# Local attention on one core: the closing feed-forward product moved to the next repeat, and the gates behind the third tile's scores

## The chip, the core and the metric

The kernel runs on one core of a Trainium2 chip. The metric is the device time of one execution in microseconds (us). Five engines work in parallel, each with its own instruction queue: PE (TensorE, matrix products and transposes into PSUM), DVE (VectorE), ACT (ScalarE), POOL (GpSimd) and SP (SyncE, which here issues all data transfers). They meet only at semaphores; within one engine everything runs in the order written.

## What is computed

The program has two parts. The first (up to about 1171 us of the span) is a mixture layer that the change does not touch. The second is a transformer of 6 layers over 8 sequences of 512 tokens, width 128, with 16 heads of 64 and local attention in windows of 32 keys, of which each query window sees its own and the one before:

```
def attn_layer(x, Wqkv, qs, ksc, Wo):
    q, k, v = split(x @ Wqkv)                       # 16 heads of 64
    q = l2norm(q) * qs;  k = l2norm(k) * ksc
    q = rotate(q, scale);  k = rotate(k, 1 / scale)
    return local_attention(q, k, v) @ Wo            # window 32

def ffn_layer(x, g, bln, W1, b1, W2, b2):
    xn = layernorm(x) * g + bln
    a, gate = split(xn @ W1 + b1)
    return a * gelu(gate) @ W2 + b2

for i in range(6):
    x = attn_layer(shift_tokens(x), ...) + x
    x = ffn_layer(shift_tokens(x), ...) + x
```

## The kernel before

`transformer` (line 1199) does the second part. One repeat (here: a trip) is one sequence in one layer, `it = l * 8 + s`; the program loops over the 6 layers and has the 8 sequences written out, so 48 trips run, of about 67 us each. The residual stream of all sequences lies in `state`, channels on partitions. A trip works on four tiles of 128 tokens, `t` = 0 to 3.

Nothing is scheduled by a planner. The list `BODY` (line 190) is the order, written by hand, and **every engine walks the same list**: at each name it does its own share of the step or passes on. The names are:

- `qk.t.j`: product of tile `t` with one of four column blocks of the query and key weights (PE, line 1535). DVE multiplies it with the rotary tables into `cs` (L1749), ACT squares it (L1629), DVE sums the squares per head (L1703), POOL adds the two halves of `cs` (L1409).
- `n.t`: the norms of tile `t`: DVE's last sum of squares and a clamp (L1731), ACT's logarithm and exponential (L1612, L1613), then POOL scales four blocks into `qk` (L1418).
- `t.t.j`: PE transposes those blocks (L1540), ACT copies them to `qTl` and `kTl` (L1640, L1642).
- `v.t.j`: value products (L1535), copied by ACT to `vl` (L1631); SP moves rows of `vl` into `vw` (lines 1328 to 1342). At `v.3.1` POOL copies the next sequence's stream to `xw` (L1427).
- `sa.t`, `s.t.p`: mask and scores of a tile in two halves (PE, L1498 and L1464); DVE takes the maximum and subtracts it (L1761, L1716), ACT exponentiates (L1619).
- `w.t`: DVE sums and inverts (L1723, L1736), POOL weighs (L1435). `pt.t.k`: PE transposes the probabilities (L1545), ACT copies (L1645). `oa.t`, `o.t.p`: output products (L1479), copied by ACT (L1647).
- `y`: output projection (L1552), added to `state` by DVE into `xm` (L1767). `xt`, `xn`: the layer norm's transposes (L1558, L1568).
- `gate.c`, `up.c`: three chunks of the hidden products (L1573). ACT applies gelu to the gate (L1659), DVE multiplies with `up` into `hf` (L1787). `y2`: closing product of `hf` with `w2l` (L1577), added by DVE to `xm` and stored in `state` (L1790).

A trip is skewed: it runs projections and early tiles of its own sequence, while the third and fourth tile's attention (`t.3`, `s.3`, `o.2`, `o.3`), `y` and the feed-forward layer belong to the sequence before (`rest_at` picks its slot).

Results leave PE through a `Ring` of the 8 PSUM banks: each product takes the next bank, and PE first waits for the reader of the product eight places earlier in the list (`readers`, `take`). Moving a name thus also moves who waits for whom.

ACT's gelu is in another function table than exponential and logarithm; where they alternate, an `ACT_TABLE_LOAD` stands between. After the loop a second block works through `OF_LAST` (line 206), the rest of the last sequence; the steps `f.s` there add and store the output. Before the loop DVE clears `kTl` and `oTl` (L1685) and then writes `tiled` (L1690), for which PE waits.

## Time and profile before

| | us |
|---|---|
| median of three runs | 4505.05 |
| the three runs | 4504.26 to 4511.89 |
| the profiled execution, its own time | 4507.19 |
| its span from first to last instruction | 4505.3 |
| PE busy | 4309.6 (96%) |
| DVE busy | 3286.9 (73%) |
| ACT busy | 2757.4 (61%) |
| POOL busy | 2181.4 (48%) |

A busy PE is not a PE at its peak, since an f32 matmul's end is modelled and overlaps the next one's start. What a step costs PE is the distance from its start to the start of the next step. The mean granted clock of TensorE is 0.994 of full.

### The profile page before, as it was taken

How to read it: one execution, taken by the hardware profiler on the slowest of the kernel's cores; microseconds unless marked ns; L12 is line 12 of the kernel's file. 1: busy time of each engine (PE TensorE's matmuls, PEld its weight loads, DVE VectorE, ACT ScalarE, POOL GpSimd, SP SyncE). 2: the span in 40 equal slices, each digit the busy share in tenths (PEclk: the TensorE clock that was granted, in tenths of full speed). 3: DMA queues.
4: the chain of work that ended last, by engine and by line, in shares of the span. 5: the costliest groups of instructions: out<-in, count | busy, mean ns of one | idle time of the engine just before them, and what ended most of it. 6: DMA issues, size and time to landing. Idle time of an engine off the chain costs nothing. (4 is left out here: it accounts for less than half of the span.)

```text
span 4505.3 us, 172609 instructions
## 1 busy us (share of the span) xinstructions
PE 4309.6 (96%) x68826; PEld 2563.6 (57%) x68826; DVE 3286.9 (73%) x5789; ACT 2757.4 (61%) x5467; POOL 2181.4 (48%) x1993
## 2 busy tenths in 40 slices
PE   8999999998799999999999999999999999999998
PEld 4555555555455655655555555555555555556554
DVE  5666666665687777777777777777777777777775
ACT  4544555544566666666666666666666666666664
POOL 0000000000366666666666766666766766666763
PEclk9999999999999999999999999999999999999998
DMA  1000000000111112111121112211122111221112
GB/s 44 4 8 6 8 8 4 8 6 4 55 53 51 46 46 71 46 49 50 43 74 48 45 49 61 56 48 47 48 58 59 49 45 48 64 53 49 50 44 80
DMA packets 145061, 189.72 MB, mean 42 GB/s; under 512 B 34151, under 2 KB 66298, under 8 KB 144250
## 3 DMA queue, kind: packets, MB, share of 16 engines
q1 hardware_dynamic: 144250, 178.39, 14.6%
q8 instruction: 572, 9.37, 0.9%
q14 instruction: 239, 1.96, 0.1%
HBM read 29.39 MB, written 4.19 MB: 7 GB/s over the span
## 5 line engine op out<-in xcount | busy, mean ns | idle before, releaser
L1409 POOL TENSOR_TENSOR cs<-cs 128x512 f32<-128x512 f32 x768 | 977.4, 1276 | 534.0 <-DVE cs L1749 531.3
L1535 PE MATMUL psum<-wqkv,xw 128*128 128x512 f32 x2304 | 1191.2, 609 | 24.1 <-DVE tiled L1690 15.6
L1749 DVE TENSOR_TENSOR cs<-psum,rots 128x1024 f32<-128x1024 f32 x768 | 933.8, 1221 | 236.6 <-PE psum L1535 225.5
L1418 POOL TENSOR_TENSOR qk<-cs,rn 128x512 f32<-128x512 f32 x768 | 776.6, 1042 | 330.3 <-ACT rn L1613 294.6
L1629 ACT ACTIVATE sq<-psum 128x512 f32<-128x512 f32 x768 | 459.0, 598 | 623.4 <-DVE cs L1749 591.8
L1442 POOL MEMSET tiled<- 128x128 bf16 x1 | 0.2, 204 | 1165.3 <-POOLq L524 1165.3
L1703 DVE TENSOR_REDUCE ss<-sq 128x8 f32<-128x512 f32 x768 | 520.0, 677 | 7.0
L1479 PEld LDWEIGHTS psum<-pT,vw 64*64 64x64 f32 x18624 | 400.4, 135 | 194.6 <-issue 194.2
L1540 PEld LDWEIGHTS psum<-ident,qk 128*128 128x128 f32 x3088 | 355.2, 141 | 230.6 <-issue 166.8
L1535 PEld LDWEIGHTS psum<-wqkv,xw 128*128 128x128 f32 x2304 | 368.6, 190 | 188.2 <-issue 164.4
L1540 PE MATMUL psum<-ident,qk 128*128 128x128 f32 x3088 | 444.9, 277 | 24.6 <-POOL qk L1418 17.8
L1479 PE MATMUL psum<-pT,vw 64*64 64x32 f32 x18624 | 445.4, 221 | 12.3 <-issue 11.0
L1435 POOL TENSOR_TENSOR probl<-probl,rs 128x512 f32<-128x512 f32 x386 | 394.4, 1043 | 52.3 <-DVE rs L1736 52.1
L1479 PE MATMUL psum<-pT,vl 64*64 64x32 f32 x6208 | 394.0, 219 | 0.0
L1464 PEld LDWEIGHTS psum<-kTl,qTl 64*32 64x32 f32 x24704 | 304.1, 105 | 147.8 <-issue 136.4
L1464 PE MATMUL psum<-kTl,qTl 64*32 64x64 f32 x24704 | 345.4, 223 | 12.6 <-issue 12.4
L1552 PE MATMUL psum<-oTl,wol 128*128 128x512 f32 x784 | 351.2, 601 | 0.6 <-DVE cs L1758 0.5
L1761 DVE TENSOR_REDUCE negmaxl<-psum 128x8 f32<-128x512 f32 x386 | 248.3, 685 | 128.1 <-PE psum L1464 127.8
L1619 ACT ACTIVATE probl<-probl 128x512 f32<-128x512 f32 x386 | 233.8, 629 | 161.4 <-DVE probl L1716 160.5
L1631 ACT COPY vl<-psum 128x512 f32<-128x512 f32 x384 | 223.0, 581 | 178.4 <-PE psum L1535 177.8
L1479 PEld LDWEIGHTS psum<-pT,vl 64*64 64x64 f32 x6208 | 326.3, 135 | 0.0
L1573 PE MATMUL psum<-x2T,w1l 128*114 128x512 f32 (+1 forms) x588 | 287.2, 612 | 0.4 <-ACT x2T L1635 0.4
(205 smaller groups left out, 6744.3 us busy)
## 6 DMA issues: line engine op xcount, KB each, us to landing
vw<-vl SPq DMA_DIRECT2D x768, 128.0 KB, 2.4
vw<-vl SPq DMA_DIRECT2D x672, 64.0 KB, 2.0
wqkv<-in_wqkv SPq DMA_DIRECT2D x42, 256.0 KB, 3.8
wol<-in_wol SPq DMA_DIRECT2D x7, 512.0 KB, 4.1
w1l<-in_w1l SPq DMA_DIRECT2D x7, 341.0 KB
xin<-in_x SPq DMA_DIRECT2D x9, 256.0 KB, 2.8
xr<-in_x SPq DMA_DIRECT2D x8, 256.0 KB, 2.8
sums<-sumout SPq DMA_DIRECT2D x8, 256.0 KB, 2.3
```

What stands on the lines that cost most here:

```text
L1409: summed_rot.done(nc.gpsimd.tensor_tensor(own, own, halves(cs[:, t % 2, j, 1, :])[:, :, ::-1, :], ALU.add), at)
L1418: rotated.done(nc.gpsimd.tensor_tensor(qk[:, j, :].rearrange("p (h c) -> p h c", c=EL), cs[:, t % 2, j, 0, :].rearrange("p (h c) -> p h c" ...
L1435: weighed.done(nc.gpsimd.tensor_tensor(p, p, r.unsqueeze(2).to_broadcast([P, 8, WK]), ALU.mult), (t, k))
L1464: last[p] = nc.tensor.matmul(banks[p][WIN * w:WIN * w + WIN, c * WK:(c + 1) * WK], qTl[rows, t % 2, c, WIN * w:WIN * w + WIN], kTl[rows, c ...
L1479: last[p] = nc.tensor.matmul(banks[p][64 * half:64 * half + 64, k * P + WIN * w:k * P + WIN * w + WIN], values(t, w, p)[:, c * EL:(c + 1) ...
L1535: last = nc.tensor.matmul(ps[:, :], xw[:, t * P:(t + 1) * P], wqkv[:, col:col + BANK], start=True, stop=True)
L1540: last = nc.tensor.transpose(ps[:, c * P:(c + 1) * P], qk[:, at[1], c * P:(c + 1) * P], ident[:, :])
L1552: last = nc.tensor.matmul(ps[:, :], wol[:, c, :], oTl[:, c, :], start=(c == 0), stop=(c == PAIRSL - 1))
L1573: last = nc.tensor.matmul(ps[0:CW[t], :], w1l[:, col:col + CW[t]], x2T[:, :], start=True, stop=True)
L1629: squared.done(nc.scalar.activation(sq[:, n % 2, :], ps[:, :], ACT.Square), at)
L1703: summed.done(V.tensor_reduce(ss[:, piece[0] % 2, 8 * j:8 * j + 8], sq[:, j % 2, :].rearrange("p (h c) -> p h c", c=EL), AX.X, ALU.add), p ...
L1749: parts.done(V.tensor_tensor(cs[:, t % 2, j, :, :].rearrange("p i (h c) -> p i h c", c=EL), twice, by_head, ALU.mult), at)
```

## The change

The closing product `y2` becomes `y2.0` and stands behind `qk.0.3 n.0` of the next trip; it closes the sequence before the one it closed until now, so it writes another slot (`closed_at`) and its weights `w2l`, `b2l` are loaded apart from the others, after it has read the old ones. At the top of the trip `t.3.3` and `qk.0.2` change places. At the end `v.3.1` goes ahead of the third tile's scores `s.2`, `n.3` directly behind them, and all three gates behind that. The last part gets one `y2` more, since two sequences are still open there. A third memset on DVE clears `hf`.

```diff
-MADE = 21
+MADE = 22
 BODY = [step(name) for name in """
-    qk.0.0 t.3.0 qk.0.1 t.3.1 t.3.2 qk.0.2 t.3.3 qk.0.3 n.0 pt.2.0 qk.1.0 sa.3
+    qk.0.0 t.3.0 qk.0.1 t.3.1 t.3.2 t.3.3 qk.0.2 qk.0.3 n.0 y2.0 pt.2.0 qk.1.0 sa.3
...
-    qk.3.3 sa.2 v.3.0 gate.0 s.2.0 s.2.1 gate.1 up.0 gate.2 v.3.1 w.2 oa.1
-    up.1 up.2 n.3 o.1.0 o.1.1 y2
+    qk.3.3 sa.2 v.3.0 v.3.1 s.2.0 s.2.1 n.3 gate.0 gate.1 w.2 up.0 gate.2 oa.1
+    up.1 up.2 o.1.0 o.1.1
...
-OF_LAST = (turn(3) + turn_probs(2) + score(3) + final(0) + [("w", 3)] + ...
-           + ... + hidden_chunks() + final(6) + [("y2",)] + final(7))
+OF_LAST = (turn(3) + [("y2", 0)] + turn_probs(2) + score(3) + final(0) + [("w", 3)] + ...
+           + ... + hidden_chunks() + final(6) + [("y2", 1)] + final(7))
...
+    def closed_at(l, s, which):
+        if which or s > 1:
+            return bass.ds(B - 1 if which else s - 2, 1)
+        past = (l * B + TRIPS - 1) // TRIPS
+        return bass.ds(B - past if s else B - past - past, 1)
+
+    closing_loads = lambda l, s: (l * B + s + B - 2) // B + 1
...
-            for j in range(1, 6):
+            for j in range(1, 4):
+                load_qkv(slice(0, 1), j)
+            load_closing(slice(0, 1))
+            for j in range(4, 6):
                 load_qkv(slice(0, 1), j)
...
-                left.wait(sp, it, "state")
+                hidden.wait(sp, it, 2)
                 settle(sp, passed)
                 load_ffn(one)
-                with sp.Fori(1, B - 1) as s:
+                move_values(it + 1, 0)
+                left.wait(sp, it + 1, (0,))
+                settle(sp, passed)
+                load_closing(one)
+                for t in range(1, T):
+                    move_values(it + 1, t)
+                with sp.Fori(2, B - 1) as s:
...
-                    left.wait_before(pool, it, "state")
+                    left.wait_before(pool, it, (0,))
...
-                if key == ("f", B - 1, 0):
-                    left.wait(pe, it, "state")
+                if key in (("f", B - 2, 0), ("f", B - 1, 0)):
+                    left.wait(pe, it, (at[0] - (B - 2),))
...
-                    hidden.wait(pe, it, 2)
+                    pe.wait_ge(w2_loaded, closing_loads(l, s) * (16 * W2_LOADS))
+                    wait_made(hidden, pe, it, 2, t == 0)
...
-                for dst in (kTl[:, :, :], oTl[:, :, :]):
+                for dst in (kTl[:, :, :], oTl[:, :, :], hf[:, :, :]):
                     V.memset(dst, 0.0).then_inc(made, 1)
-                dve.wait_ge(made, 11)
+                dve.wait_ge(made, 12)
```

How this moves instructions shows in the programs' own rows (source line, instruction, output and inputs, shape). Rows of line 77, 82, 134 and 151 are waits.

PE around the top of a trip, before; the first row is `y2`, the last ones stand ahead of `sa.3`:

```order
L1577 MATMUL psum<-hf,w2l 128x512 x3
L1535 MATMUL psum<-wqkv,xw 128x512
L1540 MATMUL psum<-ident,qk 128x128 x4
L1535 MATMUL psum<-wqkv,xw 128x512
L1540 MATMUL psum<-ident,qk 128x128 x8
L1535 MATMUL psum<-wqkv,xw 128x512
L1540 MATMUL psum<-ident,qk 128x128 x4
L1535 MATMUL psum<-wqkv,xw 128x512
L77 ISA
L1545 MATMUL psum<-ident,probl 128x128 x4
L1535 MATMUL psum<-wqkv,xw 128x512
L134 REGISTER_ALU x2
```

The same place after the change, from `qk.0.1` to the mask of `sa.3`:

```order
L1560 MATMUL psum<-wqkv,xw 128x512
L82 REGISTER_ALU
L1565 MATMUL psum<-ident,qk 128x128 x12
L1560 MATMUL psum<-wqkv,xw 128x512 x2
L77 ISA
L1600 REGISTER_ALU
L1603 MATMUL psum<-hf,w2l 128x512 x3
L1570 MATMUL psum<-ident,probl 128x128 x4
L77 REGISTER_ALU
L1560 MATMUL psum<-wqkv,xw 128x512
L134 REGISTER_ALU x2
L1523 MATMUL psum<-maskw,tiled 32x512 x8
```

The closing product moved from ahead of the trip's first product to between the four blocks of tile 0 and `pt.2.0`; the last transpose `t.3.3` moved one product up.

ACT near the end of a trip, before, from the copy of `v.3.0` to the second gelu:

```order
L1631 COPY vl<-psum 128x512
L77 REGISTER_ALU
L1659 ACT_TABLE_LOAD
L1659 ACTIVATE gel<-psum,b1l 114x512
L77 REGISTER_ALU
L1619 ACT_TABLE_LOAD
L1619 ACTIVATE probl<-probl 128x8x64
L77 REGISTER_ALU
L1619 ACTIVATE probl<-probl 128x8x64
L77 REGISTER_ALU
L1659 ACT_TABLE_LOAD
L1659 ACTIVATE gel<-psum,b1l 114x512
```

The same place after, from the copy of `v.3.1` to the first gelu:

```order
L1657 COPY vl<-psum 128x512
L77 REGISTER_ALU
L1645 ACTIVATE probl<-probl 128x8x64
L77 REGISTER_ALU
L1645 ACTIVATE probl<-probl 128x8x64
L77 REGISTER_ALU
L1638 ACTIVATE lns<-ssc 128x32
L151 REGISTER_ALU
L1639 ACTIVATE rn<-lns,lnt 128x32
L77 REGISTER_ALU
L1685 ACT_TABLE_LOAD
L1685 ACTIVATE gel<-psum,b1l 114x512
```

The exponentials and the norms of tile 3 now come first and the three gelus last, and two of four table loads are gone.

POOL in the same stretch, before, from the copy to `xw`:

```order
L1427 COPY xw<-state 128x513
L77 REGISTER_ALU
L1435 TENSOR_TENSOR probl<-probl,rs 128x512 x2
L77 REGISTER_ALU x2
L1418 TENSOR_TENSOR qk<-cs,rn 128x512
```

After:

```order
L1452 COPY xw<-state 128x513
L77 REGISTER_ALU x2
L1443 TENSOR_TENSOR qk<-cs,rn 128x512
L77 REGISTER_ALU
L1443 TENSOR_TENSOR qk<-cs,rn 128x512
L77 REGISTER_ALU
L1443 TENSOR_TENSOR qk<-cs,rn 128x512
L77 REGISTER_ALU
L1443 TENSOR_TENSOR qk<-cs,rn 128x512
L77 REGISTER_ALU
L1460 TENSOR_TENSOR probl<-probl,rs 128x512 x2
```

The scaling of tile 3 now stands ahead of the weighing of tile 2.

## Rows read from the trace of the kernel before

**Rows 1.** Stretch of 47 trips: length, busy time of each engine, clock, transfers.
```profile
1254.24:4441.16 3186.92, 3110.44 (x58369) 1879.88 (x58367) 2493.41 (x3924) 2083.99 (x3849) 2117.50 (x1926) 1.00 0.20 52
```
**Rows 2.** PE's waits in those trips: waiting line, releaser, total, times, longest.
```profile
PE psum L1498 <- ACT kTl L1642: 26.5, 46, 1.8
PE psum L1540 <- POOL qk L1418: 17.3, 70, 0.4
PE psum L1464 <- issue: 12.4, 27, 1.1
PE psum L1479 <- issue: 8.4, 20, 0.9
```
**Rows 3.** PE's timeline over one trip's turn: start, length, line, [idle before, releaser].
```profile
2391.13 1.88 PE L1535 MATMUL psum<-wqkv,xw 128*128 128x512 f32 x4
2392.94 0.41 PE L1498 MATMUL psum<-maskw,tiled 64*32 64x512 bf16 x8
...
2404.43 2.85 PE L1577 MATMUL psum<-hf,w2l 114*128 114x512 f32 x6
2407.11 1.02 PE L1535 MATMUL psum<-wqkv,xw 128*128 128x512 f32 x2
2407.97 0.60 PE L1540 MATMUL psum<-ident,qk 128*128 128x128 f32 x4
2408.40 1.02 PE L1535 MATMUL psum<-wqkv,xw 128*128 128x512 f32 x2
...
2412.73 1.02 PE L1535 MATMUL psum<-wqkv,xw 128*128 128x512 f32 x2
2414.28 0.41 PE L1498 MATMUL psum<-maskw,tiled 64*32 64x512 bf16 x8 [0.52 <-ACT kTl L1642]
...
2418.52 1.38 PE L1540 MATMUL psum<-ident,qk 128*128 128x128 f32 x8
...
2420.67 1.02 PE L1535 MATMUL psum<-wqkv,xw 128*128 128x512 f32 x2
```
**Rows 4.** DVE's timeline in the same stretch.
```profile
2398.07 1.28 DVE L1716 TENSOR_TENSOR probl<-psum,negmaxl 128x512 f32<-128x512 f32 x2
...
2407.31 1.51 DVE L1790 SCALAR_TENSOR_TENSOR state<-psum,b2l,xm 64x512 f32<-64x512 f32 x2 [2.18 <-PE psum L1577]
2408.86 2.36 DVE L1749 TENSOR_TENSOR cs<-psum,rots 128x1024 f32<-128x1024 f32 x2
...
2416.04 0.19 DVE L1731 TENSOR_TENSOR ssc<-ss,least 128x32 f32<-128x32 f32 x1
```
**Rows 5.** ACT's timeline in the same stretch.
```profile
2399.56 1.15 ACT L1619 ACTIVATE probl<-probl 128x512 f32<-128x512 f32 x2
2400.72 1.28 ACT L1659 ACT_TABLE_LOAD   x1
2402.02 1.27 ACT L1659 ACTIVATE gel<-psum,b1l 114x512 f32<-114x512 f32 x2
...
2405.42 0.32 ACT L1613 ACTIVATE rn<-lns,lnt 128x32 f32<-128x32 f32 x1
...
2413.46 0.58 ACT L1642 COPY kTl<-psum 128x512 f32<-128x512 f32 x1
```
**Rows 6.** POOL's timeline in the same stretch.
```profile
2405.96 4.05 POOL L1418 TENSOR_TENSOR qk<-cs,rn 128x512 f32<-128x512 f32 x4 [2.05 <-ACT rn L1613]
...
2417.08 4.05 POOL L1418 TENSOR_TENSOR qk<-cs,rn 128x512 f32<-128x512 f32 x4 [1.06 <-ACT rn L1613]
```
**Rows 7.** Timelines of DVE and PE ahead of the first trip.
```profile
1180.35 3.47 DVE L1685 MEMSET oTl<- 128x4096 f32 x1 [0.80 <-issue]
...
1185.74 2.07 PE L1535 MATMUL psum<-wqkv,xw 128*128 128x512 f32 x2 [15.62 <-DVE tiled L1690]
```
**Rows 8.** Timelines of SP and PE between the last trip and the closing part.
```profile
4442.32 0.54 SPq L1338 DMA_DIRECT2D vw<-vl  x1
...
4449.18 3.65 PE L1540 MATMUL psum<-ident,qk 128*128 128x128 f32 x16 [5.17 <-DVEq L66]
```

More of the change, by code:

```diff
@@ L203, in final @@
     return [("f", s, half) for half in range(2)]
-OF_LAST = (turn(3) + turn_probs(2) + score(3) + final(0) + [("w", 3)] + output(2) + final(1) + final(2) + turn_probs(3) + output(3)
-           + final(3) + [("y",), ("xt",)] + final(4) + [("xn",)] + final(5) + hidden_chunks() + final(6) + [("y2",)] + final(7))
+OF_LAST = (turn(3) + [("y2", 0)] + turn_probs(2) + score(3) + final(0) + [("w", 3)] + output(2) + final(1) + final(2) + turn_probs(3) + output(3)
+           + final(3) + [("y",), ("xt",)] + final(4) + [("xn",)] + final(5) + hidden_chunks() + final(6) + [("y2", 1)] + final(7))
 TRIPS = DEPTH * B
@@ L1187, in __init__ @@
         self.qkv_loaded = [ctx.enter_context(nc.semaphore(f"qkv_loaded{j}")) for j in range(6)]
-        self.o_loaded, self.ffn_loaded, self.rot_loaded, self.made = (
-            ctx.enter_context(nc.semaphore(n)) for n in ("o_loaded", "ffn_loaded", "rot_loaded", "made"))
+        self.o_loaded, self.ffn_loaded, self.w2_loaded, self.rot_loaded, self.made = (
+            ctx.enter_context(nc.semaphore(n)) for n in ("o_loaded", "ffn_loaded", "w2_loaded", "rot_loaded", "made"))
         self.vmoved = [ctx.enter_context(nc.semaphore(f"vmoved{t}")) for t in range(T)]
@@ L1203, in transformer @@
     mv, lnv, rstd, x2, x2T, gel, hf, qkv_loaded = buf.mv, buf.lnv, buf.rstd, buf.x2, buf.x2T, buf.gel, buf.hf, buf.qkv_loaded
-    o_loaded, ffn_loaded, rot_loaded, made, vmoved = buf.o_loaded, buf.ffn_loaded, buf.rot_loaded, buf.made, buf.vmoved
+    o_loaded, ffn_loaded, w2_loaded, vmoved = buf.o_loaded, buf.ffn_loaded, buf.w2_loaded, buf.vmoved
+    rot_loaded, made = buf.rot_loaded, buf.made
     def sem(name):
@@ L1240, in transformer @@
     hidden = steps("hidden", lambda key: key[1] if key[0] == "up" else None)
-    left = steps("left", last_of("y2", "state"))
+    left = steps("left", place("y2"))
     squared = steps("squared", place("qk"))
@@ L1285, in readers @@
             return [(hidden, at[0])]
-        return [(left, "state")]
+        return [(left, at)]
     ring = Ring(sem("filledl"), [(key, readers(key)) for key in order if key[0] not in ("n", "w", "sa", "oa")])
@@ L1312, in load_ffn @@
                 sp.dma_start(w1l[:, :], io["w1l"][layer].rearrange("l p n -> p (l n)")).then_inc(ffn_loaded, 16)
-                for dst, name in ((lng, "lng"), (lnb, "lnb"), (b2l, "b2l")):
+                for dst, name in ((lng, "lng"), (lnb, "lnb")):
                     sp.dma_start(dst[:, :], io[name][layer].rearrange("l p -> p l")).then_inc(ffn_loaded, 16)
@@ L1316, in load_ffn @@
                 for c, m in enumerate(CW):
-                    sp.dma_start(w2l[0:m, c, :], io["w2l"][layer][:, at:at + m, :].rearrange("l p d -> p (l d)")
-                                 ).then_inc(ffn_loaded, 16)
                     for a in range(2):
@@ L1321, in load_ffn, with load_closing @@
                                      .rearrange("l p -> p l")).then_inc(ffn_loaded, 16)
+                    at += m
+            def load_closing(layer):
+                sp.dma_start(b2l[:, :], io["b2l"][layer].rearrange("l p -> p l")).then_inc(w2_loaded, 16)
+                at = 0
+                for c, m in enumerate(CW):
+                    sp.dma_start(w2l[0:m, c, :], io["w2l"][layer][:, at:at + m, :].rearrange("l p d -> p (l d)")
+                                 ).then_inc(w2_loaded, 16)
                     at += m
@@ L1394, in _ @@
                 sp.wait_ge(qkv_loaded[j], DEPTH * 16 + 16)
-        FFN_LOADS = 4 + 3 * 3
+        FFN_LOADS, W2_LOADS = 3 + 2 * 3, 4
         @block.gpsimd
@@ L1790, in read @@
                     last = unshift(lambda a, b, d: V.scalar_tensor_tensor(
-                        out=state[a:b, rest_at(l, s), d:N + d].rearrange("p s n -> p (s n)"), in0=ps[a:b, :],
+                        out=state[a:b, closed_at(l, s, t), d:N + d].rearrange("p s n -> p (s n)"), in0=ps[a:b, :],
                         scalar=b2l[a:b, 0:1], in1=xm[a:b, d:N + d], op0=ALU.add, op1=ALU.add))
-                    left.done(last, "state")
+                    left.done(last, at)
             if last_part:
```

## The prediction

> **What bounds the kernel now.** I read three views in this order. First the table by stretches: over 47 trips, from the first product of the second trip to the start of the last closing product, PE is busy 3110.4 of 3186.9 us and DVE, the next, 2493.4, all at the full granted clock [rows 1]. So a trip takes 67.8 us, and only what PE executes and what it waits for count; an edit on another engine is worth nothing unless PE waits for it. Second PE's waits: two have an engine as releaser, the mask of `sa.3` for ACT's copy into `kTl` and the transposes `t.0.j` for POOL's scaled blocks; the others are "issue", PE waiting for nothing that the profile names, inside the long runs of small score and output matmuls [rows 2]. Third the timeline, to size the two. A pair of products with a mask behind takes 2392.94 - 2391.13 = 1.81, so one product with a mask behind takes 1.81 - 0.86 = 0.95, where 0.86 is a plain product (2407.97 - 2407.11). Ahead of `sa.3` it takes 2414.28 - 2412.73 = 1.55: **wait A is 0.60 us**. The three transposes `t.0.0` to `t.0.2` should take 3 x 0.435 = 1.31 (one is 2408.40 - 2407.97) and take 2420.67 - 2418.52 = 2.15: **wait B is 0.84 us** [rows 3]. The waits view counts less because it starts where a matmul's modelled end lies.
>
> **Why they are there.** DVE stands idle 2.18 us for the closing product, moves it out in 1.51 until 2408.8, and only then takes the first products of the trip, which PE had finished at 2407.97 and 2409.26 [rows 3, 4]. Everything behind is late by that: `cs`, ACT's squares, ACT's copy of `t.3.3`, which stands in ACT's queue behind the square of `qk.0.2` and ends at 2414.04 [rows 5], which is wait A, and the clamp of tile 0 at 2416.04 [rows 4], ACT's norm and POOL's four blocks from 2417.08 on, 1.01 us each [rows 6], which is wait B.
>
> **The change, top of the trip.** PE's work is the same 2.68 us (2407.11 - 2404.43 [rows 3]), in another place. I walk the new order in the trace's times. PE ends `o.1.1` at 2404.4 as before and starts `qk.0.0` at once. DVE, by then done with `hf`, takes the four products as they come: 2405.5, 2406.7, 2408.9, 2410.1 or soon after, with sums between, and has the clamp of tile 0 ready near 2413.4 instead of 2416.2. `t.3.3` leaves PE at 2407.9 and is no longer queued behind a square that is late; ACT has copied it by about 2410. `sa.3` comes at 2404.4 + four products, four transposes, 2.68, one transpose group and one product = 2413.6, over 3 us later: wait A is gone. DVE moves `y2.0` out from 2413.4 to 2414.9 and takes `qk.1.0` at 2414.9, 1.3 earlier than now. ACT's norm is out at 14.0, POOL's blocks end at 2415.1, 16.1, 17.1 and 18.1; PE wants the third at 2418.8: wait B is gone, with 1.7 in hand. `y2.0` itself waits for nothing: `hf` is complete at 2405.1, its weights were loaded a layer or a trip ago, its bank was freed by the square of `qk.0.0`, at 2407.3 against 2409.6. From there on every engine repeats the old schedule 1.44 earlier, since DVE is back to waiting for PE from `qk.1.2` on.
>
> **The change, end of the trip.** The new queue on ACT is exponentials, norm of tile 3, table load, three gelus, table load, two copies. The scores are centred at 2399.3 as now [rows 4]; the exponentials no longer wait for a table and end at 2399.9, the norm at 2400.9 (now 2405.7), the load at 2402.2, the gelus, 0.64 to 0.69 each, at 2402.9, 2403.5 and, behind DVE's first `hf`, 2404.3, the second load at 2405.6, the copies of `o.1` at 2406.2 and 2406.7, where they are now [rows 5]. Who waits for that: PE, through the ring. `qk.0.0` takes the bank of `gate.0` at 2404.4 (freed 2402.9, 1.5 in hand), `t.3.0` that of `gate.1` (1.8), `t.3.1` that of `gate.2` (2.3), `qk.0.2` that of `o.1.0` (1.7). POOL scales tile 3 from 2400.9 to 2405.0, wanted from 2405.3 on, and weighs tile 2 until 2407.0, wanted at 2412.3. The smallest margin is 1.5 us. Two of four table loads go, 2.56 us of ACT, worth nothing by themselves, since no one waits for ACT there. SP loads the closing weights in the second trip of a layer, 4 transfers issued in about 1.8 us, ahead of value moves that are wanted 20 us later.
>
> **The sum.** Waits A and B over 48 trips: 42 trips x 1.44 = 60.5, and six at a layer's start, where a longer turn of the loop lets DVE catch up, at about 1.1: **-66.7**. One more closing product, because the first trip runs an empty one: **+2.7**. The memset of `hf`: 1536/4096 x 3.47, on DVE's path to `tiled`, for which PE waits [rows 7]: **+1.3**. Between loop and closing part all engines meet, and the last is SP, whose eight value moves of tile 3 start at 4442.32, behind ACT's copy of `v.3.1`, 1.16 after the end of `o.1.1` [rows 8]; that copy is early now: **-1.0**. In the closing part `y2.0` stands openly between the transposes and the scores, where the old last one was hidden under the meeting: 2.7 at the full clock, 5.2 if the half clock holds, since the 16 matmuls there take 3.44 for 1.75 [rows 8]; the clock comes back soon after, so **+3.2**. Last the issue waits. They sit in runs of small matmuls at places fixed by the code (12.4 + 8.4 us in 47 trips [rows 2]); a PE that waits less gives them less time to catch up. Bounds: they shrink with the longer stretch of large matmuls ahead of `sa.3`, -4, or wait B's 0.84 comes back in full, +37. A and B lie mostly 2 us and more ahead of those places, so I take **+3**. Sum -57.5. The span becomes 4447.8; the profiled execution was 2.1 us above the median, so I set the sum against the median: 4505.05 - 57.5 = **4447.5 us**.
>
> The Trainium skill, "Runtime: NRT & Kernel Launch", section "Instruction fetch mechanics", says that instructions are streamed in blocks of 256 and that crossing a block costs something "mostly hidden". By it the term of +3 would be 0 and the time 4444.5. The trace speaks against "hidden": the waits on issue lie inside runs without any semaphore, up to 1.1 us long [rows 2]. I keep the row.
>
> **The rivals.**
> 1. *The issue waits take part of it back.* For: they fall on the next long run of small matmuls, `oa.2` stands right behind wait B and shows none today, perhaps because of B. Against: 47 waits in 47 trips over eight differently placed copies of the trip, so one copy more or two would be hit. At half of the gain of B and A: 4505 - 33 + 9 = about 4478; with one or two copies more, 4455.
> 2. *Only wait A goes.* If DVE, which now has `y2.0` between tile 0 and tile 1, or POOL, which now weighs tile 2 ahead of the first `cs` sum, is later than walked by over 1.7 us, B stays: 48 x 0.60 = 29 less, 6 more: 4482.
> 3. *Slower: the gelus are too late.* The place is PE's wait at `qk.0.0` for the bank of `gate.0`. Its margin is 1.5 us; ACT has there five things in a row that all hang on DVE's centring. Beyond 1.5 each 0.1 us costs 4.7 us over the trips, and from 1.5 + 1.2 = 2.7 us on the change loses. At 3.5 late: 47 x 2.0 - 57.5 = +36: 4541. In the last trip of a layer DVE is some 0.9 us later through its tables, and even there it holds.
> 4. *Nothing moves*, because a new wait, as that for the closing weights, stands in each trip: 4505. The loads happen once in eight trips, so hardly.
> 5. *Better*: the issue waits shrink too and the closing part keeps the full clock: 4437.
>
> **Chances.** Forecast 0.68 (4440 to 4455), rival 5 0.07, rival 1 0.12, rival 2 0.08, rival 3 0.04, rival 4 0.01. The range leaves out 2 in 10: it goes from 4438, the forecast with the issue waits at their lower bound and the meeting as walked, to 4470, which takes in the smaller half of rival 1. Measurements of this kernel tell 0.2% apart, some 9 us. Faster 0.95, same 0.01, slower 0.04.
>
> **What would show it.** In the profile after: PE's waits list no `kTl` at the mask and no POOL at the transposes; a common trip takes 65.4 us instead of 66.8; DVE no longer waits for the closing product; ACT has 2 table loads a trip; PE starts the first trip 1.3 later. If PE waits for a gelu at `qk.0.0`, rival 3 is at work; if issue grows from 21 to 40 us or more, rival 1; if the transposes of tile 0 still wait, rival 2. The forecast is wrong at its root if the trips stay at 66.8 with both waits gone.

## The result and the profile after

The changed kernel takes 4482.05 us (median of 4 runs, 4477.13 to 4483.74); the kernel before, run beside it, 4506.68 us (4504.26 to 4511.89). The ratio is 0.9942 with a 95% interval of 0.9925 to 0.9959: faster by 24.6 us (0.6%; the interval excludes no change), where 57.5 were forecast. The time lies above the range. The profiled execution has a span of 4481.0 us against 4505.3, so 24.3 us less are to be explained.

First PE's waits between 1260 and 4430 us of the changed kernel, the view of [rows 2] (line and releaser, total, times, longest). Line 1560 is a product, 1565 a transpose, 1504 and 1489 the small output and score matmuls:

```profile
PE psum L1560 <- issue: 19.5, 5, 4.3
PE psum L1504 <- issue: 16.8, 32, 1.0
PE psum L1565 <- DVEq L66: 6.7, 1, 6.7
PE psum L1489 <- issue: 5.1, 13, 0.7
```

Neither the mask nor the transposes of tile 0 wait for another engine: both waits of [rows 2] that the prediction set out to remove, 26.5 and 17.3 us in that view, are gone. The waits on issue inside small matmuls are what they were, 16.8 + 5.1 = 21.9 us against 12.4 + 8.4 = 20.8. The 6.7 us at `DVEq` are the meeting ahead of the closing part. New is the first row: **five waits of 3.9 us on average at a product**, one at each turn of PE's layer loop.

The stretch that answers to [rows 1], from the first product of the second trip to the end of `o.1.1` of the last:

```profile
1260.80:4417.56 3156.76, 3107.09 (x58380) 1892.43 (x58374) 2498.47 (x3925) 1970.46 (x3759) 2112.94 (x1927) 1.00 0.20 53
```

It is 3156.76 us long instead of 3186.92, and PE is busy 3107.1 us in it instead of 3110.4: of the 30 us that went, 27 are idle time.

Now a common trip. PE's timeline from `qk.0.0` of a trip on (start, length, line, operation; an idle time before it would stand in brackets):

```profile
1797.99 1.13 PE L1560 MATMUL psum<-wqkv,xw 128*128 128x512 f32 x2
...
1803.28 2.74 PE L1603 MATMUL psum<-hf,w2l 114*128 114x512 f32 x6
...
1806.30 1.02 PE L1560 MATMUL psum<-wqkv,xw 128*128 128x512 f32 x2
1807.25 0.41 PE L1523 MATMUL psum<-maskw,tiled 64*32 64x512 bf16 x8
...
1811.49 1.47 PE L1565 MATMUL psum<-ident,qk 128*128 128x128 f32 x12
1812.80 1.02 PE L1560 MATMUL psum<-wqkv,xw 128*128 128x512 f32 x2
```

`y2.0` stands at 5.3 us into the trip. `sa.3` follows its product after 1807.25 - 1806.30 = 0.95, the time that the prediction gave for a product with a mask behind and no wait. The three transposes ahead of 1812.80 take 1.31, as they should without a wait. The other engines in that trip, ACT, then DVE, then POOL:

```profile
1794.37 1.28 ACT L1685 ACT_TABLE_LOAD   x1
1795.66 1.26 ACT L1685 ACTIVATE gel<-psum,b1l 114x512 f32<-114x512 f32 x2
1797.16 0.69 ACT L1685 ACTIVATE gel<-psum,b1l 113x512 f32<-113x512 f32 x1 [0.24 <-DVE hf L1813]
```
```profile
1806.96 0.19 DVE L1757 TENSOR_TENSOR ssc<-ss,least 128x32 f32<-128x32 f32 x1
1807.07 1.51 DVE L1816 SCALAR_TENSOR_TENSOR state<-psum,b2l,xm 64x512 f32 x2
```
```profile
1807.99 4.05 POOL L1443 TENSOR_TENSOR qk<-cs,rn 128x512 f32<-128x512 f32 x4 [1.07 <-ACT rn L1639]
```

ACT ends its gelus 0.14 us ahead of PE's next trip and DVE moves `y2.0` out with no wait for PE. POOL's third block of tile 0 is ready 3.04 after 1807.99, at 1811.0, and PE takes it at 1812.36. All of this is the order that the prediction walked, and its times hold within 0.3 us.

### The profile page after: what moved, and what is told of

The parts are those of the page before. It is cut to its first block and busy times, and to the rows that moved or that the text cites. A ratio compares the mean times of both kernels' runs of the same rounds, so it can differ in the third digit from the quotient of the medians.

```text
span 4481.0 us, 172692 instructions
## 1 busy us (share of the span) xinstructions
PE 4311.3 (96%) x68832; PEld 2578.3 (58%) x68832; DVE 3294.7 (74%) x5792; ACT 2639.2 (59%) x5371; POOL 2176.5 (49%) x1993
## 3 DMA queue, kind: packets, MB, share of 16 engines
q8 instruction: 572, 9.37, 0.9%
HBM read 29.39 MB, written 4.19 MB: 7 GB/s over the span
## 5 line engine op out<-in xcount | busy, mean ns | idle before, releaser
L1560 PE MATMUL psum<-wqkv,xw 128*128 128x512 f32 x2304 | 1187.4, 614 | 36.8 <-issue 19.5
L1565 PE MATMUL psum<-ident,qk 128*128 128x128 f32 x3088 | 423.2, 278 | 6.7 <-DVEq L66 6.7
```

Of the source, the lines that this page charges most:

```text
L1560: last = nc.tensor.matmul(ps[:, :], xw[:, t * P:(t + 1) * P], wqkv[:, col:col + BANK], start=True, stop=True)
L1565: last = nc.tensor.transpose(ps[:, c * P:(c + 1) * P], qk[:, at[1], c * P:(c + 1) * P], ident[:, :])
```

## Where the other 33 us went: a ledger

I cut every trip at the masks, at the first transpose of tile 0, at `oa.2` and at `y`, in both traces, and took the length of each piece after minus before; the 2.68 us of `y2` are booked as moved, not as lost or won. Over 47 trips, without `y2`:

| piece of the trip | 41 common trips | 6 trips at a layer's start | 5 trips at a layer's end | sum |
|---|---|---|---|---|
| top to `sa.3` (wait A) | -0.61 each | +0.79 each | as common | -20.0 |
| `sa.3` to the transposes of tile 0 | -0.01 | -0.66 | as common | -4.5 |
| transposes to `oa.2` (wait B) | -0.71 | -0.20 | as common | -30.2 |
| `oa.2` to `sa.2` (small matmuls) | by the place of the trip in its layer, -0.7 to +1.1 | | | +10.2 |
| `sa.2` to the next trip's top | about 0 | about 0 | **+2.70** | +13.6 |

The sum is -31 us, where the prediction's terms gave -62.6. The rest of the span: PE starts the first trip 6.4 us later, the 48th trip up to the end of `o.1` is 0.9 longer (it has the one `y2` more, 2.7, and gained 1.8), the meeting is 1.2 shorter and the closing part 0.5 longer. Together that is -24.3.

The -0.66 of the second line is neither wait A nor wait B. In the first trip of layers 1 to 5 the kernel before waited on issue inside the scores `s.3`, by 0.5 to 1.3 us (the longest at 3913.69), which the changed kernel does not.

The last column but one is the surprise. These are PE's rows where a layer ends, of the kernel before and of the changed one (in brackets the idle time ahead):

```profile
2267.90 2.85 PE L1577 MATMUL psum<-hf,w2l 114*128 114x512 f32 x6
2272.52 1.12 PE L1535 MATMUL psum<-wqkv,xw 128*128 128x512 f32 x2 [1.77 <-issue]
```
```profile
2264.02 0.22 PE L1504 MATMUL psum<-pT,vl 64*64 64x32 f32 x1
2268.51 2.07 PE L1560 MATMUL psum<-wqkv,xw 128*128 128x512 f32 x2 [4.27 <-issue]
```

Before, PE stood still for 1.8 us at the turn, and had 2.7 us of `y2` to execute up to that; after, it stands still for 4.3 us behind the last small matmul of `o.1`. The five stops are 1.42, 1.77, 1.28, 1.23 and 1.82 us before, 3.90, 4.27, 3.83, 3.98 and 3.54 after. And the product behind the stop, two matmuls, takes 2.07 us instead of 1.12. The table by stretches of the changed kernel (length; busy time of PE, PEld, DVE, ACT, POOL; granted clock as a share of full speed, DMA share, GB/s) shows why:

```profile
2263.00:2265.00 2.00, 1.24 (x65) 1.02 (x64) 1.45 (x3) 1.74 (x4) 2.00 (x3) 1.00 0.08 17
2265.00:2267.00 2.00, 0.00 (x0) 0.00 (x0) 0.71 (x1) 1.99 (x3) 2.00 (x3) 0.82 0.18 45
2267.00:2269.00 2.00, 0.49 (x1) 0.50 (x2) 0.00 (x0) 0.32 (x1) 0.69 (x1) 0.50 0.43 115
2269.00:2271.00 2.00, 2.00 (x5) 0.86 (x5) 0.28 (x1) 0.00 (x0) 0.00 (x0) 0.50 0.53 124
```

The clock falls from 2.4 to 1.2 GHz during the stop and stays there behind it; such stretches lie at all five turns and last 3.4 to 6.8 us, and the kernel before has none in its trips. What PE waits for in the stop these rows do not name, but PE's own queue does. Asked by source line, the branch of the layer loop stands in the trace with its duration (nanoseconds, shortest, median and longest of six). First the kernel before, then the changed one:

```profile
L1584 PEldq COMPARE_BRANCH  x6: 83/3608/4037, 1724.4 to 4441.2; - x6
```
```profile
L1610 PEldq COMPARE_BRANCH  x6: 83/3688/4097, 1726.4 to 4417.3; - x6
```

The sixth branch of each kernel leaves the loop and takes 0.08 us. The five that go back take 3.5 to 4.0 us before and 3.4 to 4.1 after: **the branch costs the same in both kernels**, and PE's next product starts 0.5 us behind its end. What differs is how much PE still has to execute when the branch begins: 2.7 to 2.8 us before, 0.3 after. The stop is the branch, plus 0.5, less that.

The transfers of instruction code tell what the branch is busy with. Each on queue q8 moves 16 KB (the page after counts 572 of them with 9.37 MB), and near a turn the view of the DMA queues, asked for a tenth of a microsecond (two tenths for the kernel before), has exactly one in that window. After, in 2264.9 to 2265.0; before, in 2269.1 to 2269.3 (transfers, MB, share of 16 engines in that window):

```profile
q8 instruction: 1, 0.02, 94.6%
```
```profile
q8 instruction: 1, 0.02, 40.0%
```

From the start of that transfer to PE's next product it is 3.6 us after and 3.3 before, and over all ten turns of both kernels 2.8 to 3.6. It starts 1.0 to 1.6 us behind the start of the branch: after, 0.6 to 0.7 us behind the point at which PE has run dry, before, 1.1 to 1.8 us ahead of it. I read that so: PE's instructions are taken up ahead of their execution, the branch at the loop's end is met while the matmuls queued ahead of it are still to be executed, and their execution hides the fetch. The 128 small matmuls of `o.1` hide 0.3 us of it; `y2` hid 2.7. The Trainium skill says so in words: "Runtime: NRT & Kernel Launch", section "Instruction fetch mechanics", warns that a taken branch whose target is not in the window that has been fetched has to wait for a transfer of the target, a stall. The trace agrees and puts 3.5 to 4.3 us on it, or 1.2 to 1.8 with large matmuls queued ahead. I had weighed only what that section says of crossing a block.

## The experiments

Theory 1: the change removed waits A and B as walked, and the turn of PE's loop took back some 25 us, by the stop and by the half clock behind it (by the ledger it is 24: 13.5 at the ends of the layers, the rest at the tops behind them). The rivals: the stop is a wait for the next layer's data, the end order is not what matters, or the waits on issue moved.

**Large matmuls last.** The changed kernel with `o.1` ahead of the last three gate and up products, so that 2.8 us of large matmuls stand at the branch:

```diff
-    qk.3.3 sa.2 v.3.0 v.3.1 s.2.0 s.2.1 n.3 gate.0 gate.1 w.2 up.0 gate.2 oa.1
-    up.1 up.2 o.1.0 o.1.1
+    qk.3.3 sa.2 v.3.0 v.3.1 s.2.0 s.2.1 n.3 gate.0 gate.1 w.2 oa.1 up.0
+    o.1.0 o.1.1 gate.2 up.1 up.2
```


> The changed kernel, with o.1 drawn ahead of gate.2, up.1 and up.2, so that six large matmuls (2.9 us) are the last thing in a trip instead of 128 small ones. Theory 1 (the turn of the layer loop costs PE a stop of some 4 us before new instructions are there; what is still queued for PE covers it, and the small output matmuls cover almost nothing; the stop of 4 us then drops the granted clock to half for 3 to 7 us): the five stops shrink from 3.5-4.3 us each to 1.0-1.5, the clock stays full at the turns, and the time falls by 5 x 2.6 + 5 x 1.5, some 20 us, to about 4462. Rival (the stop is a wait for the next layer's weights or for another engine): it stays at 3.5 to 4.3 us, time 4480 to 4485.

Measured 4465.97 us (4459.99 to 4468.93), ratio 0.9906 (0.9890 to 0.9923): 16 us less than the changed kernel. Every engine walks the new order, but in the common trips it changes nothing: cut by the same ledger, of the 15.9 us that the 47 trips lost, the five layer ends give 9.4 and the tops behind them 5.5. PE's waits at the product at a layer's start:

```profile
PE psum L1560 <- ACT gel L1685: 8.8, 4, 2.4
PE psum L1560 <- issue: 2.5, 1, 2.5
```

They sum to 11.3 us instead of 19.5, and the half clock in the trips shrinks from 23.9 to 6.8 us. Each is still 1.9 to 2.5 us, more than the 1.2 to 1.8 before. The releaser in the first row is a coincidence: at 2258.83, say, that gelu had ended 0.9 us earlier. The branch and the transfers tell it. The branch is longer here, 4.4 to 5.0 us, of which the large matmuls hide 3.0. Two blocks are fetched together, at 2254.1 and 2254.7, the second takes some 2 us, and PE goes on at 2258.83, 4.7 us behind the first. Over the five turns it is 4.6 to 4.9 from the first of the two.

**One half of the change alone.** First the product moved and the trip's end left as it was (in the changed kernel):

```diff
-    qk.3.3 sa.2 v.3.0 v.3.1 s.2.0 s.2.1 n.3 gate.0 gate.1 w.2 up.0 gate.2 oa.1
-    up.1 up.2 o.1.0 o.1.1
+    qk.3.3 sa.2 v.3.0 gate.0 s.2.0 s.2.1 gate.1 up.0 gate.2 v.3.1 w.2 oa.1
+    up.1 up.2 n.3 o.1.0 o.1.1
```


> Only the top of the trip is changed (y2.0 behind n.0, t.3.3 ahead of qk.0.2); the end keeps the old order of gates, v.3.1 and n.3, without y2. Theory: PE's waits for ACT's kTl copy and at the transposes of tile 0 are gone, but the norms of tile 3 come 5 us later than in the changed kernel, so POOL's blocks of tile 3 end at about 2.6, 3.6, 4.6 and 5.6 us after PE ends o.1, and the transposes t.3.j, wanted from 0.9 us on, wait 2.5 us in each trip: 4505 + 48 x (2.5 - 1.3) = about 4565. Rival (the end of the trip has slack and its new order is worth nothing): about 4482, as the whole change.

Then the new end with the product left where it was (in the kernel before):

```diff
-    qk.3.3 sa.2 v.3.0 gate.0 s.2.0 s.2.1 gate.1 up.0 gate.2 v.3.1 w.2 oa.1
-    up.1 up.2 n.3 o.1.0 o.1.1 y2
+    qk.3.3 sa.2 v.3.0 v.3.1 s.2.0 s.2.1 n.3 gate.0 gate.1 w.2 up.0 gate.2 oa.1
+    up.1 up.2 o.1.0 o.1.1 y2
```


> Only the end of the trip is changed (v.3.1, n.3 and the gates in their new places); y2 stays at the end of its own trip. Theory: the waits at sa.3 and t.0.j stay, because they come from DVE taking y2 ahead of the new trip's products, and y2 now waits about 0.7 us for the last hf: 48 x 0.7 = 34 us slower than before, about 4538; the turns of the layer loop stop PE for 1.4 us and the clock stays full there, as before. Rival (the gates' new place, with two table loads less, is what gains): about 4480.

Measured 4591.9 us (ratio 1.0186, 1.0169 to 1.0203) and 4550.1 us (1.0092, 1.0076 to 1.0109). Each half alone makes the kernel slower, by 82 and 41 us against the kernel before run beside them (4509.49), and both together make it faster. The leading waits of PE, of the first and of the second:

```profile
PE psum L1565 <- POOL qk L1443: 80.9, 81, 1.7
PE psum L1560 <- issue: 19.4, 5, 4.1
```
```profile
PE psum L1577 <- DVE hf L1787: 33.5, 46, 1.5
PE psum L1498 <- ACT kTl L1642: 26.1, 47, 1.8
PE psum L1540 <- POOL qk L1418: 17.5, 65, 0.4
```

With `n.3` late, POOL's scaling of tile 3 comes too late for `t.3.0` once `y2` no longer stands between; with the gates late, `hf` comes too late for a `y2` at the trip's end, while waits A and B stay as they are. So the norm ahead of the gates is what makes room for the moved product, and the moved product what makes room for late gates. The stop at the turn is in the first (19.4 us, five times), which has small matmuls last, and small in the second, which ends with `y2`: the stop goes with the last work of the trip.

**The code shifted.** In the changed kernel, 128 semaphore increments ahead of PE's loop; the loop itself is untouched:

```diff
+            for _ in range(128):
+                settle(pe, passed)
             with pe.Fori(0, DEPTH) as l:
```


> The changed kernel with 128 semaphore increments more on PE ahead of the loop, which shifts all of the loop's PE instructions by half a block of 256. Theory (the issue waits inside runs of small matmuls are fetches of the next block of instructions, at places fixed by the code): they move to other trips of the eight (now the fifth to the seventh hold most of them), their sum stays 22 us within 10, time 4475 to 4492. Rival (they hang on data, semaphores or on the transfers of that trip): same trips, same sums, time unchanged within 3 us.

Measured 4494.82 us (4490.29 to 4499.53). The increments cost 19.7 us ahead of the first trip (1192.17 to 1211.89), more than I had given them; without them the time is 4475. From the first trip's start to the last's it is 3157.0 us against 3158.7 in the changed kernel. Inside the trips the waits on issue moved, from the sixth and seventh to the first three of a layer, and their sum (with two lines too small to show here) is 18.6 us instead of 21.9, while the turns took 24.2 instead of 19.5:

```profile
PE psum L1560 <- issue: 24.2, 5, 5.6
PE psum L1504 <- issue: 15.2, 29, 1.1
```

The turns are longer for the reason seen above: at four of the five, two blocks are fetched together, and the branch takes 4.6 to 5.4 us there, 3.4 at the other.

The place of these waits can be counted. Take every recorded instruction of PE, matmuls, weight loads and those of its queue, and number them from the first. In the first layer of both kernels each wait of over 0.25 us inside small matmuls lies at place 193 or 194 of a block of 256, though the shifted code has 128 instructions more ahead of it. So they move over the work and keep their place in the blocks, which is what fetches of the next block would do, as expected.

The same two lines added to the kernel before:

> The kernel before with 128 semaphore increments ahead of PE's loop, which shift the whole of its loop code; read against the kernel before as the shifted changed kernel was read against the changed one. The increments themselves delay the first trip by about 19.7 us; what counts is the time from the first trip's start to the start of the last trip, 3189.7 us in the kernel before. Theory (the waits on issue depend on where the code of a small-matmul run lies, and the kernel before is placed luckily; written out, where each trip lies elsewhere, it needed 3215.6): the stretch grows by 8 to 26 us, with waits at other places of the trips, and the time is 4535 to 4550. Rival (a written-out program is slower for another reason): the stretch stays within 4 us of 3190 and the time is about 4527.

Measured 4525.43 us (4521.0 to 4533.32); without the increments some 4506, no change, and the stretch from the first trip's start to the last's is 3192.7 us against 3189.7. The rival holds: in both kernels this shift, the only one tried, changed which trips wait on issue and hardly how much all of them do (22.0 us in the two lines of [rows 2] for 20.8).

**PE's loop written out.** If the branch is the cause, fewer branches cost less. Two layers in each round of PE's loop, then all six with no loop:

```diff
-            with pe.Fori(0, DEPTH) as l:
-                for s in range(B):
...
+            with pe.Fori(0, DEPTH // 2) as h:
+                for u in range(2):
+                    l = h * 2 + u
+                    for s in range(B):
```


> The changed kernel with PE's layer loop written out for two layers (three rounds of the loop instead of six, so 2 turns instead of 5); the work, its order and every other engine's program are as in the changed kernel. Theory 1 (the loop's turn on PE costs a stop of about 3.9 us and then about 2 us of work at half clock, since only small, quickly executed matmuls are queued ahead of it): 3 of the 5 stops are gone, 4482 - 3 x 6 = about 4464, and PE goes from layer 1 to 2, 3 to 4 and 5 to 6 with no stop over 1.2 us. Rival (the stop is a wait for something else of the next layer, its weights or another engine's turn): the stops stay at all five places and the time stays at about 4482. Should the code's new places move issue waits, their sum of 22 us stays within some 10.

```diff
-            with pe.Fori(0, DEPTH) as l:
+            for l in range(DEPTH):
```


> The changed kernel with all six layers of PE's program written out, no loop on PE; every other engine as in the changed kernel. Theory 1: no stop at a layer's start, no half clock behind it: 4482 - 5 x 6 = about 4452, which is the time that the prediction should have given had it walked the turn rightly without a loop. Rival (something else of the next layer): about 4482, and the stop keeps 3.5 to 4.3 us. Second rival (code that runs only once is fetched more slowly than code of a loop, so that waits on issue grow with it): the stops go, but the waits on issue in the score and output matmuls grow beyond 30 us and the time stays above 4465.

Two layers: 4464.23 us (4459.04 to 4467.94), ratio 0.9894 (0.9878 to 0.9911), 18 us less than the changed kernel, as theory 1 said; that it agrees to the microsecond is luck, with executions 9 us apart. The stops are at the two turns only, 4.32 and 4.19 us, and the half clock with them; layers 1, 3 and 5 begin with none. That excludes a wait for a layer's data. No loop: 4464.99 us (4462.92 to 4467.42), ratio 0.9899 (0.9883 to 0.9916). The stops are gone, but the time is no lower than with two turns and misses 4452 by 13. Its waits of PE:

```profile
PE psum L1504 <- issue: 23.6, 42, 1.2
PE psum L1489 <- issue: 9.7, 20, 0.7
...
PE psum L1603 <- ACT sq L1655: 3.0, 4, 0.9
```

In the ledger against the changed kernel the ends of the five last trips of a layer give 17.8 us and the tops behind them 6.2. Two things take part of it back. The waits on issue in small matmuls are 33.3 us in this view instead of 21.9. And the other engines have turns of their own at a layer's start: where PE no longer stops, it waits for ACT's square, and wait B is back in the first trip of layers 1 to 5 (0.4 to 0.9 us each, 4 in all). The second rival of this run, that written-out code waits more, got the numbers right (over 30 us, and 4465); its reason is not shown, since the code transfers on q8 are no slower (1.13 us on average against 1.10) nor more in number (552 against 572).

The same with the memset of `hf` moved from DVE to POOL:

```diff
-            for dst in (qTl[:, :, :, :], xm[:, :], qk[:, :, :], probl[:, :, :, :, :], pT[:, :, :]):
+            for dst in (qTl[:, :, :, :], xm[:, :], qk[:, :, :], probl[:, :, :, :, :], pT[:, :, :], hf[:, :, :]):
...
-                for dst in (kTl[:, :, :], oTl[:, :, :], hf[:, :, :]):
+                for dst in (kTl[:, :, :], oTl[:, :, :]):
```


> As the one before, with the memset of hf on POOL instead of DVE, where the first trip's start waited for it. Theory: 1.3 to 1.6 us less than that kernel, about 4450; PE starts the first trip that much earlier. Rival (POOL's memsets are what the first trip waits for too, since POOL is slower at them): no gain, or a loss of up to 3 us.

Measured 4464.91 us, no difference. The start of the first trip varies by more than the memset's 1.3 us between executions of the same opening code: 1186.88 with the memset on DVE and no loop, 1187.34 with large matmuls last, 1192.33 with two layers. So the time says nothing on the memset either way. The wait of PE's first product for `tiled` does: it is 16.77 us with the memset on DVE and 15.17 with it on POOL, 1.6 less, as the theory had it. The part ahead of it ended 3.2 us later in this execution, and a gain of 1.6 is below what the medians tell apart.

**The kernel before, written out.** All six layers, and three layers in each round:

```diff
-            with pe.Fori(0, DEPTH) as l:
+            for l in range(DEPTH):
```
```diff
+            with pe.Fori(0, DEPTH // 3) as h:
+                for u in range(3):
+                    l = h * 3 + u
```

> The kernel before, with all six layers of PE's program written out. There PE stopped 1.4 us at each turn, 1.67 over what the products there take, with 2.7 us of the closing product queued ahead. Theory 1: only 5 x 1.7 = 8 us go, 4506.7 - 8 = about 4498, against 30 in the changed kernel: the closing product at the trip's end hid most of the turn. Rival (a written-out PE program is worth the same in both, because it gains elsewhere): about 30 less, 4477.

> The kernel before with PE's loop written out for three layers: one turn instead of five, the trip's order unchanged. Theory (a turn costs the kernel before 1.7 us, and the 20 us that the fully written-out program lost have to do with the loop being gone altogether): four turns less, 4507.4 - 4 x 1.7 = about 4500. Rival (every layer written out costs issue waits of its own, which in the changed kernel are hidden by what the turns give back): about half or more of those 20 us show already, 4512 to 4525.

Measured 4531.73 us (ratio 1.0042, 1.0028 to 1.0056) and 4512.77 us (1.0008, 0.9999 to 1.0018). Neither theory had the first: fewer turns bring the kernel before nothing, and no loop at all makes it 20 us slower. With three layers the ends of the last trips gain 1.25 us each, and the tops of the first trips lose 1.16 each: there PE only comes earlier to engines whose own turns are late. Of the four waits that [rows 2] lists the first kernel has two as they were (26.7 for 26.5, 12.1 for 12.4) and more of the two others (25.0 for 17.3, 18.0 for 8.4). Of PE's waits, fully written out, then with three layers:

```profile
PE psum L1540 <- POOL qk L1418: 25.0, 78, 0.4
PE psum L1479 <- issue: 18.0, 41, 1.0
PE psum L1464 <- issue: 12.1, 32, 0.8
```
```profile
PE psum L1540 <- POOL qk L1418: 13.6, 53, 0.4
PE psum L1479 <- issue: 12.7, 25, 1.2
```

The waits view starts at a matmul's modelled end. By the distance from one start to the next, all gaps of over 0.08 us inside small matmuls come to 38.0 us in 47 trips of the kernel before and to 61.5 fully written out, which is most of the 26.0 us that those trips grew. Why a program without any loop waits more on issue stays open. One shift of the code did not do it, and the transfers are no longer (1.15 us on average against 1.14).

**Few turns and large matmuls last.** The order of the first experiment, with two and with three layers written out:

```diff
+    o.1.0 o.1.1 gate.2 up.1 up.2
...
+            with pe.Fori(0, DEPTH // 2) as h:
...
+            with pe.Fori(0, DEPTH // 3) as h:
```

> The changed kernel with PE's loop written out for two layers and up.2 last in the trip. The records of code transfers show that PE starts again 3.0 to 3.7 us after the transfer of the loop's first block starts, and that this transfer starts when PE's sequencer comes to the branch, 0.6 us after PE has run dry in the changed kernel and about 2 us before that where large matmuls are still queued. Theory: 2 stops of about 2 us instead of 2 of 4.3, without the half clock behind them, so some 2 x 5 = 8 us less than the two-layer kernel's 4464, about 4456; the half clock in the loop is gone. Rival (what remains is code placement): between 4460 and 4470.

> As the one before with three layers written out, so one turn instead of two. Theory: 2 to 3 us less from the turn, about 4454. Rival (the other engines' turns show where PE's is gone, and the code's places cost more the more of it there is, as in the fully written-out kernel at 4465): 4458 to 4465.

Measured 4456.46 us (4452.08 to 4459.96), ratio 0.9889 (0.9872 to 0.9905), and 4455.65 us (4450.2 to 4458.3), ratio 0.9883 (0.9867 to 0.9900). Both beat the changed kernel by 26 us and the kernel before by 51 to 52. Against two layers alone (0.9894, 0.9878 to 0.9911) the intervals overlap, so the gain from the large matmuls on top of that isn't shown by the times; from the first trip's start to the last's it is 7.5 us in one execution of each. The two stops of the first are 1.90 and 2.84 us, the one of the second 1.00. The half clock did not go altogether in the first, against the expectation: where a layer begins without a turn, PE now waits up to 2.1 us for ACT's square, and the clock falls for 3.4 us, three times:

```profile
1731.00:1735.00 4.00, 1.93 (x3) 0.75 (x3) 3.95 (x4) 2.56 (x6) 2.51 (x2) 0.80 0.01 2
```

In the second the waits of PE begin with:

```profile
PE psum L1504 <- issue: 17.3, 30, 1.4
PE psum L1603 <- ACT sq L1657: 9.5, 5, 2.5
```

At a layer's start the bound is now the other engines' turn. In this kernel, at 1730, where PE has no branch, these are the records of DVE's own:

```profile
L1830 DVEq COMPARE_BRANCH  x1: 68/68/68, 1728.0 to 1728.0; - x1
L1830 DVEq FUSED_REGOPS  x1: 63/63/63, 1731.4 to 1731.4; - x1
```
```profile
1731.71 2.36 DVE L1777 TENSOR_TENSOR cs<-psum,rots 128x1024 f32<-128x1024 f32 x2 [3.03 <-PE psum L1560]
```

The view puts the 3.03 us down to PE, whose first product had been ready since about 1727; from DVE's branch to its next instruction it is 3.4 us. In the kernel before, the changed one, the one with no loop on PE and this one, that distance is 2.4 to 3.1 us on ACT, 2.8 to 4.0 on DVE and 3.0 to 3.5 on POOL. This kernel and the three-layer form of the kernel before have one turn of PE each: 4455.65 against 4512.77 is 57 us, and over 47 trips they differ by 3131.54 - 3191.67 = -60.1 us, where the prediction's terms for the trips gave -62.6. It is no pure comparison, since the order at the end differs too, but it is near to what the change is worth where PE's turn plays no part. Fully written out the pair gives 4531.7 - 4465.0 = 67 us, with the same orders as before and after, and part of that is the unexplained loss of the kernel before.

## Why the prediction was wrong, step by step

**What bounds the kernel, and waits A and B: right.** Both waits are gone in every common trip, for the reasons given, and the two experiments with one half each show that neither half would have done it.

**The failed step** is the first sentence of the walk at the top of the trip: "PE ends `o.1.1` at 2404.4 as before and starts `qk.0.0` at once." In 43 of 48 trips it does; at the five turns of the layer loop it does not. I walked one trip in the middle of a layer and applied it to all. The turn was in the trace of before, as stops of 1.2 to 1.8 us behind `y2`, and my sum held it constant; I used a layer's start only to take 1.1 instead of 1.44 for the gain there. That `y2` was also the work behind which most of PE's branch was hidden, and that moving it away uncovers the fetch, I did not see. Size: 5 x 2.7 = 13.5 us at the ends, and 6 x 1.7 = 10.1 at the tops behind them and in the first trip (+0.79 - 0.20 = +0.59 where -1.1 was forecast), together some 24 of the 33 us. The large-last order gave back 16 and two layers per round 18.

**Wait B over-sized.** The transposes gave all of the 0.84, 1.31 us instead of 2.15, but the trip kept only 0.71 of it. Behind the last transposes of tile 0 the small output matmuls now come later, by 0.15 us in nearly every trip; before, then after:

```profile
2421.53 0.60 PE L1540 MATMUL psum<-ident,qk 128*128 128x128 f32 x4
2422.06 0.32 PE L1479 MATMUL psum<-pT,vw 64*64 64x32 f32 x8
```
```profile
1813.66 0.60 PE L1565 MATMUL psum<-ident,qk 128*128 128x128 f32 x4
1814.34 0.32 PE L1504 MATMUL psum<-pT,vw 64*64 64x32 f32 x8
```

That is 0.53 and 0.68 us. The kernel before took 0.71 there too in the three trips without wait B, so the wait had covered this much of what stands behind it. What PE does in these 0.15 us no view names. With wait A at 0.61 as forecast, a common trip gained 1.33 where 1.44 was forecast: 41 x 0.11 = 4.5 us.

**The issue waits.** +3 was forecast. The pieces from `oa.2` to `sa.2` took +10.2, and `s.3` at the layers' starts gave 6 x 0.66 = 4.0 back: +6.2, so 3 more. In PE's waits their sum grew by 1.1 only, so rival 1 in its strong form did not come, and the condition set for it, 40 us in the same view without the turns, was not met. The reasoning that a PE that waits less for others waits more for code has the right sign; the shift shows that the place changes where, not how much.

**The start.** The memset took 1.34 us as forecast (1.3), and the first trip started 6.4 us later in this execution:

```profile
1188.91 1.34 DVE L1711 MEMSET hf<- 128x1536 f32 x1 [0.27 <-issue]
```
```profile
1192.17 1.22 PE L1560 MATMUL psum<-wqkv,xw 128*128 128x512 f32 x1 [17.21 <-DVE tiled L1716]
```

The opening part, which is the same in both, had ended 4.8 us later, and the wait for `tiled` was 1.6 longer (17.21 for 15.62). Kernels with the same opening started the first trip at 1186.9 to 1192.4, so those 4.8 us are scatter of an execution, not the change.

**The meeting and the closing part.** SP's first value move came at 4417.78 behind `o.1.1`, PE started the closing part at 4424.36, 6.8 us behind it where it was 8.0 [rows 8]: -1.2 for a forecast of -1.0. The closing part took 0.5 more, not 3.2:

```profile
4424.36 3.65 PE L1565 MATMUL psum<-ident,qk 128*128 128x128 f32 x16 [6.74 <-DVEq L66]
4427.80 4.00 PE L1603 MATMUL psum<-hf,w2l 114*128 114x512 f32 x6
```

The product stands openly in the part and at less than the full clock, 3.8 us, as walked; the others, which had waited for each other there, were quicker by nearly as much. Misses of 24, 4.5 and 3 us in the trips and of 5 at the start, less 3 behind them, make up the 33.

**Two slips in the arithmetic.** The waits add up to 42 x 1.44 + 6 x 1.1 = 67.1, not 66.7, and rival 1's 4505 - 33 + 9 is 4481, not 4478. The first moves the forecast by 0.4 us; the second puts the price of rival 1 at the measured time as well, and its mechanism did not happen either.

**The rivals.** Rival 2, "only wait A goes", named 4482 and the measured time is 4482.05, but its mechanism did not happen: wait B is gone. A time that agrees proves no cause; the waits view had to be read. None of the five rivals was a stop at the turn, so the range could not take it in. The sign that the prediction set for itself was "a common trip takes 65.4 us instead of 66.8": the shortest take 65.7 to 65.9, and the median of all 47 is 66.8 instead of 67.7.

## What to carry to other kernels

Ahead of a loop's branch on the engine that bounds the kernel, keep long-running instructions queued: their execution hides the branch and the fetch of the loop's first code block (3.4 to 4.1 us here), and an edit that moves the last of them away costs a stop at each turn and may drop the clock as well. A change that is walked in one iteration has to be walked at the loop's turn too, for what each moved step hides there. And where two halves of an edit each lose alone (82 and 41 us here), test them together before giving them up.

## What the runs showed of the hardware

**The turn of a loop on PE** costs 3.4 to 4.1 us, the time that the branch back stands in PE's queue, and 0.5 more to the next product; where two blocks are fetched together the branch takes 4.4 to 5.4. The branch that leaves the loop takes 0.08. From the start of the 16 KB transfer to the first product it is 2.8 to 3.6 us, and 4.5 to 5.4 with two. It was visible in full only where small matmuls stood last. ACT, DVE and POOL pay 2.4 to 4.0 us for turns of their own.

**The clock** was granted at 1.2 GHz for 3.4 to 6.8 us behind each of the stops of 3.5 to 4.3 us; behind those of 1.2 to 1.8 us in the kernel before it stayed at 2.4. Between them both happened: with large matmuls last it fell behind 1.9 and 2.5 us and not behind 2.1, 2.4 and 2.4, and in the two-layer form of that kernel it held behind turns of 1.9 and 2.8. The length of the stop alone does not decide it.

**Where small matmuls wait on issue** the distance to the next such wait is a whole number of blocks of 256 instructions of PE. In the changed kernel with no loop on PE I counted 47 waits of over 0.25 us in small matmuls, and all lie at place 193 or 194 of a block: 1, 2, 4, 5, 6, 9, 10, 11 or more blocks apart. Of matmuls, each with its weight load, that is 124, 250, 498, 624 and so on. PE's 141597 recorded instructions there are 553 blocks, and the page counts 552 transfers on q8. The Trainium skill, "Runtime: NRT & Kernel Launch", section "Instruction fetch mechanics", gives blocks of 256 instructions; the distances agree. Its "mostly hidden" does not hold in runs of small matmuls, where single waits reach 1.0 to 1.4 us.
